# A gated recurrence beside expert layers and attention: the state's decay moved to ScalarE, and the blend scanned over three elements per batch in place of two

## The chip, the core and the metric

The kernel runs on one core of one Trainium2 chip. Its time is the device time of one execution in microseconds; of the kernel before three runs are given, and one more that was profiled. TensorE (PE; its weight loads are PEld), VectorE (DVE), ScalarE (ACT) and GpSimd (POOL) each take their instructions strictly in the order in which they are written, and wait for one another through semaphores.

## What is computed

Four layers, each added to its own input, on x of 8 batches, 256 positions, 128 features. Layers 0 and 1 are mixtures of experts (a shared part, and eight experts of which two count for each position), layer 3 is causal attention with 16 heads. Layer 2 is a recurrence over the 256 positions; its state h has 128 features for each of 8 batches:

```python
leak = 1.0 - alpha
def step(h, z_t):
    gate = jax.nn.sigmoid(h @ Wh.T + z_t @ Wz.T + b)
    h_new = jnp.tanh(h * leak + gate * z_t)
    return (h_new, h_new)
_, hs = jax.lax.scan(step, h_t, jnp.swapaxes(z, 0, 1))
```

Here z is the output of layer 1, h_t starts as the condition vector, and every h is added to x before layer 3. With sigmoid(a) = 0.5 + 0.5 tanh(a/2), gate * z is 0.5 z tanh(a/2) + 0.5 z.

## The kernel before, in words

Positions are cut into eight chunks of 32. A planner writes out, slot by slot, which unit of work each engine does; a unit is for instance one 512 wide bank of an expert's hidden layer. One step of the recurrence is woven into most slots once the first chunk has been through layers 0 and 1: after that the later chunks' expert layers run beside the steps, and the first half of attention too. What is left of attention runs behind the last step. The planner's table, the slots and the queues are the same before and after the change, but for the instructions named below.

One step t, by engine, in the order in which each writes it (line numbers of the kernel before):

- TensorE multiplies the state by Wh: the state is held as a high half hhi (16 bits, two matmuls, L987) and a rest hlo (one matmul, L990), which are added into the bank that already holds z @ Wz + b. Then it does the slot's units.
- ScalarE takes tanh of that (L734, "the gate's tanh"), into d1, does the slot's units other than the late ones, waits for the scan, and writes tanh of the scan's result twice, as hhi (L746) and as the full state hs (L747). The late units (LATE: "E", the Gelu of an expert's bank, L674; "S", an exponential of attention, L724; "K" and "Q", copies of keys and queries, L693) stand behind L747, and so ahead of the gate's tanh of the next step.
- VectorE computes hlo from hs and hhi (L1270), then the decay leak * h + 0.5 z (L1272), the first half of the slot's units, the blend as a scan (L1283), and the other half of the units. A unit that is in the middle is cut in two, half on each side of the scan.

The scan keeps a running value s and for each element sets s = d0 * s + d1. With two elements for each batch, (0, tanh) and (0.5 z, leak * h + 0.5 z), the second leaves tanh * 0.5 z + leak * h + 0.5 z, which is the argument of the new state's tanh. A copy on ScalarE for each chunk (L627, unit "Z") lays 0.5 z out in d0, which holds 128 positions at a time. GpSimd clears d0 at the start (L556).

Semaphores around a step: h_hi and h_full count L746 and L747, h_lo counts L1270, gate_pre counts L990, gate_th counts L734, decay counts L1272, blend counts L1283.

Of the kernel before, what the change touches and what calls it, by code (L numbers as in the profile page):

```python
# [19 lines left out]
F32 = mybir.dt.float32  # L20
# [3 lines left out]
ACT = mybir.ActivationFunctionType  # L24
ALU = mybir.AluOpType
AX = mybir.AxisListType

P = 128
B, T, D = 8, 256, 128
# [7 lines left out]
CHUNKS = (32,) * 8  # L37
STARTS = tuple(sum(CHUNKS[:i]) for i in range(len(CHUNKS)))
NC = len(CHUNKS)
QT = 128  # L40
# [4 lines left out]
ZR = 128  # L45
# [309 lines left out]
def chunk_of(t):  # L355
    return max(i for i in range(NC) if STARTS[i] <= t)


def build(nc, x_in, small_in, up_in, down_in, rec_in, att_in, maskr_in, out):
    parts, nth, steps, bank_of, before, hg_of, hb_of, n_slots = plan()  # L360

    with ExitStack() as ctx:
        def sb(name, shape, dt=F32):
            return ctx.enter_context(nc.sbuf_tensor(name, shape, dt))
# [7 lines left out]
        x = sb("x", [P, T * B])  # L372
# [3 lines left out]
        xsp0 = sb("xsp0", [P, 2, 2, 256], F16)  # L376
# [5 lines left out]
        sel = sb("sel", [P, E, P], F16)  # L382
# [26 lines left out]
        b2 = sb("b2", [P, 2], F16)  # L409
        leak = sb("leak", [P, 1])  # L410
        warm = sb("warm", [P, 1])
        d0 = sb("d0", [P, ZR, B, 2])
        d1 = sb("d1", [P, 2, B, 2])
        hs = sb("hs", [P, T + 1, B])
        hhi = sb("hhi", [P, 2, B], F16)
        hlo = sb("hlo", [P, 2, B], F16)
# [19 lines left out]
        wm = sb("wm", [P, B, H])  # L436
        mm = sb("mm", [P, B, H])
        mneg = sb("mneg", [P, B, H], BF16)
        eimg = sb("eimg", [P, 2, 2 * QT])

        pt = hb[:, 0:NPT, :]
        avs = hg[:, 2:4, :]
        vimgd = kq[:].rearrange("p a b n -> p (a b n)").bitcast(F32).rearrange("p (b d) -> p b d", b=B)
        on = hg[:, 0:2, :].rearrange("p a (b q) -> p (a b) q", q=QT)
        onq = sb("onq", [P, 4, P])
        rden = sb("rden", [P, 2, H])
        ob = silu[:].rearrange("p a (b q) -> p a b q", b=4)

# [3 lines left out]
        cbk = [ps("cbk0"), ps("cbk1")]  # L452
        vbk = ps("vbk")
        hid = [ps(f"hid{i}") for i in range(NHT)] + [vbk] + cbk
        vps = vbk[:, 0:2 * B]
        abk = ybk
        v_of = vx[:, 0:2 * B * H * HW].rearrange("p (t b h d) -> p t b h d", t=2, b=B, h=H)

# [56 lines left out]
        def cols(c):  # L515
            return slice(STARTS[c] * B, (STARTS[c] + CHUNKS[c]) * B)
# [28 lines left out]
        @block.gpsimd  # L545
        def _(pool):
            def split_x(c):

                n = CHUNKS[c] * B
                pool.wait_ge(in_x[c], 16)  # L550
                nc.gpsimd.tensor_copy(xsp0[:, c % 2, 0, 0:n], x[:, cols(c)]).then_inc(x_hi, 1)
                pool.wait_ge(x_hi, c + 1)
                nc.gpsimd.tensor_tensor(xsp0[:, c % 2, 1, 0:n], x[:, cols(c)], xsp0[:, c % 2, 0, 0:n],
                                        ALU.subtract).then_inc(x_split, 1)

            nc.gpsimd.memset(d0[:], 0.0).then_inc(pool_set, 1)  # L556
            nc.gpsimd.memset(gt[:], 0.0).then_inc(pool_set, 1)
            nc.gpsimd.memset(spread[:], 0.0).then_inc(pool_set, 1)
            for c in (0, 1):
                split_x(c)  # L560
            nc.gpsimd.memset(vx[:], 1.0).then_inc(pool_set, 1)
            chain = [0]

            def link(ins):

                chain[0] += 1
                ins.then_inc(pool_link, 1)
                pool.wait_ge(pool_link, chain[0])

            tts, tsc = nc.gpsimd.tensor_tensor, nc.gpsimd.tensor_scalar  # L570
            for kind, *key in parts["pool"]:
                if kind == "RG":
                    c, l = key
                    k = CHUNKS[c] * B // P
                    pool.wait_ge(dve_done, nth["dve", ("RC", c, l)])
                    if c:
                        pool.wait_ge(pe_done, nth["pe", ("GT", c - 1, l)])
                    if nth["pool", ("RG", c, l)] > 1:
                        pool.wait_ge(gates_made, nth["pool", ("RG", c, l)] - 1)
                    wide = lambda a: a.rearrange("p (k o) -> p k o", o=1).broadcast_to([P, k, E])  # L580
                    tts(pick[:, l, 0:k, :], both[:, l, 0:k, 0, :], both[:, l, 0:k, 1, :], ALU.add)
                    link(tts(gr[:, 0:k, :], sg[:, l, 0:k, :], wide(rcp2[:, l, 0:k]), ALU.mult))
                    link(tts(gr[:, 0:k, :], gr[:, 0:k, :], wide(zer2[:, l, 0:k]), ALU.add))
                    link(tts(gr[:, 0:k, :], gr[:, 0:k, :], pick[:, l, 0:k, :], ALU.mult))

                    link(nc.gpsimd.tensor_copy(g2[:, l, 0:k, 0:E], gr[:, 0:k, :]))
                    tts(g2[:, l, 0:k, E:2 * E], gr[:, 0:k, :], g2[:, l, 0:k, 0:E], ALU.subtract).then_inc(gates_made, 1)

        @block.scalar
        def _(act):  # L590
# [4 lines left out]

            act.wait_ge(in_rec, 32)
            nc.scalar.activation(warm[:, 0:1], hs[:, 0, 0:1], ACT.Gelu)

            chain = [0]

            def unit(key):
# [16 lines left out]
                elif kind == "Z":  # L618
# [5 lines left out]
                    else:  # L624
                        act.wait_ge(pool_set, 1)
                    z0 = STARTS[c] % ZR
                    nc.scalar.activation(d0[:, z0:z0 + CHUNKS[c], :, 1], x[:, cols(c)].rearrange("p (t b) -> p t b", b=B),  # L627
                                         ACT.Copy, scale=0.5).then_inc(act_done, 1)
                elif kind == "MB":

                    _, i = key
# [95 lines left out]
            for s in range(n_slots):  # L727
                t = steps.get(s)
                if t is not None:

                    act.wait_ge(gate_pre, t + 1)
                    c = chunk_of(t)
                    o = (t - STARTS[c]) * B
                    nc.scalar.activation(d1[:, t % 2, :, 0], cbk[c % 2][:, o:o + B], ACT.Tanh,  # L734
                                         scale=0.5 / RS).then_inc(gate_th, 1)

                units = parts["act"][s]
                early = [k for k in units if t is None or k[0] not in LATE]
                for key in early:
                    unit(key)  # L740
                if t is not None:

                    act.wait_ge(blend, t + 1)
                    new = vps.rearrange("p (b o) -> p b o", o=2)[:, :, 1]
                    if t + 1 < T:
                        nc.scalar.activation(hhi[:, (t + 1) % 2, :], new, ACT.Tanh).then_inc(h_hi, 1)  # L746
                    nc.scalar.activation(hs[:, t + 1, :], new, ACT.Tanh).then_inc(h_full, 1)  # L747
                for key in units:
                    if key not in early:
                        unit(key)  # L750
# [245 lines left out]
        def _(dve):  # L996
# [263 lines left out]
            for s in range(n_slots):  # L1260
# [7 lines left out]
                if t:  # L1268
                    dve.wait_ge(h_full, t)
                    tts(hlo[:, t % 2, :], hs[:, t, :], hhi[:, t % 2, :], ALU.subtract).then_inc(h_lo, 1)  # L1270
                dve.wait_ge(act_done, nth["act", ("Z", chunk_of(t))])
                stt(d1[:, t % 2, :, 1], hs[:, t, :], leak[:], d0[:, t % ZR, :, 1], ALU.mult, ALU.add).then_inc(decay, 1)  # L1272

                first = [k for i, k in enumerate(units) if i < len(units) // 2]
                rest = units[len(units) // 2:]
                cut = len(units) % 2 == 1 and rest[0][0] in HALVED
# [2 lines left out]
                if cut:  # L1279
                    unit(rest[0], 0)  # L1280
                dve.wait_ge(gate_th, t + 1)
                dve.wait_ge(decay, t + 1)
                nc.vector.tensor_tensor_scan(vps, d0[:, t % ZR].rearrange("p b o -> p (b o)"),  # L1283
                                             d1[:, t % 2].rearrange("p b o -> p (b o)"), 0.0, ALU.mult,
                                             ALU.add).then_inc(blend, 1)
                if cut:
                    unit(rest[0], 1)
# [84 lines left out]
```

## Time and profile before

| what | value |
|---|---|
| median of 3 runs | 520.59 us (519.63 to 524.53) |
| the profiled execution | 519.57 us, of which the span from the first to the last instruction is 517.8 us |
| granted TensorE clock, mean of the span | 0.968 |
| gate's tanh of the first and of the last step | 45.7 us and 373.6 us into the span |
| busy: PE, DVE, ACT, POOL | 90%, 69%, 53%, 6% |

The 256 steps take the stretch from 45.7 to 373.9 us. Ahead of it the first chunk goes through the expert layers, behind it TensorE is busy with attention (from 450 to 500 us it is busy all the time). A matmul's end is modelled, so 90% is not a full TensorE.

### The profile page before, as it was taken

Reading aid. Unit: us, or ns where it says so; the run is one execution under the profiler, and the core shown is the slowest. Engines: PE = TensorE matmul, PEld = TensorE weight load, DVE = VectorE, ACT = ScalarE, POOL = GpSimd, SP = SyncE. Lnnn points to the kernel's source line nnn. Section 1 sums busy time; section 2 is a strip of 40 time slices with the busy share of each in tenths; the row PEclk is TensorE's granted clock in tenths of the full one; section 3 lists DMA queues with packets and bytes.
Section 4 is the critical chain, followed back from the end, with each engine's and each line's share of the span. In section 5 each row is a group of like instructions: output and inputs, shape, how many; then the busy total and the mean of one; then the engine's idle time right before and its main releaser. Section 6 shows DMA issues by size and latency. Waiting matters only on the chain. (4 is left out here: it accounts for less than half of the span.)

```text
span 517.8 us, 12688 instructions
## 1 busy us (share of the span) xinstructions
PE 464.6 (90%) x4202; PEld 312.7 (60%) x4202; DVE 355.4 (69%) x1562; ACT 273.0 (53%) x1112; POOL 30.7 (6%) x108
## 2 busy tenths in 40 slices
PE   3899997888999998999998878899998799999995
PEld 2667576556676676766765335566564566766662
DVE  5766887887887888778777688877533865555501
ACT  3442644644646546455455754465668544454561
POOL 7120100000200101010000000000000000000000
PEclk9999997998999999999999978999999799999997
DMA  8400000000000000000000000000000000000000
GB/s 313 187 1 1 2 0 3 2 1 2 1 2 3 1 1 3 1 2 2 1 2 2 0 1 1 3 1 3 1 22 3 1 22 3 1 1 23 2 3 21
DMA packets 4912, 8.30 MB, mean 16 GB/s; under 512 B 496, under 2 KB 3824, under 8 KB 4720
## 3 DMA queue, kind: packets, MB, share of 16 engines
q1 hardware_dynamic: 4416, 7.23, 3.9%
q8 instruction: 35, 0.57, 0.5%
q10 hardware_dynamic: 432, 0.27, 0.2%
q14 instruction: 29, 0.24, 0.2%
HBM read 6.44 MB, written 1.05 MB: 14 GB/s over the span
## 5 line engine op out<-in xcount | busy, mean ns | idle before, releaser
L822 PE MATMUL ybk<-hg,down 128*128 128x256 f32 x352 | 97.5, 401 | 2.0 <-DVE hg L1160 1.2
L968 PE MATMUL hid<-xsp,up 128*128 128x256 f16 x672 | 94.5, 281 | 3.9 <-DVE up L1046 1.6
L734 ACT ACTIVATE d<-cbk 128x8 f32<-128x8 f32 x256 | 45.8, 179 | 96.9 <-PE cbk L990 95.7
L1283 DVE TENSOR_TENSOR_SCAN vbk<-d 128x16 f32<-128x16 f32 x256 | 51.2, 200 | 34.7 <-ACT d L734 31.4
L746 ACT ACTIVATE hhi<-vbk 128x8 f16<-128x8 f32 x255 | 44.9, 176 | 53.3 <-DVE vbk L1283 52.9
L987 PEld LDWEIGHTS cbk<-hhi,wh 128*128 128x128 f16 x512 | 38.0, 99 | 54.5 <-ACT hhi L746 45.1
L968 PEld LDWEIGHTS hid<-xsp,up 128*128 128x128 f16 x672 | 60.6, 100 | 14.2 <-ACT hb L674 2.2
L822 PEld LDWEIGHTS ybk<-hg,down 128*128 128x128 f32 x352 | 60.6, 192 | 8.9 <-DVE hg L1160 2.1
L1201 DVE TENSOR_REDUCE wm<-hid 128x2 f32<-128x256 f32 (+2 forms) x94 | 50.7, 541 | 22.0 <-PE hid L881 19.8
L987 PE MATMUL cbk<-hhi,wh 128*128 128x8 f16 x512 | 51.3, 171 | 11.1 <-ACT hhi L746 9.4
L1270 DVE TENSOR_TENSOR hlo<-hs,hhi 128x8 f16<-128x8 f32 x255 | 42.8, 168 | 24.4 <-ACT hs L747 21.2
L990 PE MATMUL cbk<-hlo,wh 128*128 128x8 f16 x256 | 45.2, 176 | 14.6 <-DVE hlo L1270 6.5
L1272 DVE SCALAR_TENSOR_TENSOR d<-hs,leak,d 128x8 f32<-128x8 f32 x256 | 56.6, 221 | 0.0
L1165 DVE TENSOR_TENSOR hg<-hb,hid 128x256 f32<-128x256 f32 (+1 forms) x110 | 50.5, 460 | 7.5 <-PE hid L808 6.7
L724 ACT ACTIVATE hb<-hid,att 128x512 f32<-128x512 f32 x60 | 40.9, 688 | 26.9 <-PE hid L932 26.3
L747 ACT ACTIVATE hs<-vbk 128x8 f32<-128x8 f32 x256 | 44.4, 173 | 0.3 <-DVE vbk L1283 0.3
L990 PEld LDWEIGHTS cbk<-hlo,wh 128*128 128x128 f16 x256 | 24.6, 96 | 30.5 <-DVE hlo L1270 23.5
L674 ACT ACTIVATE hb<-hid 128x512 f32<-128x512 f32 x64 | 38.5, 603 | 3.4 <-PE hid L968 3.2
L945 PE MATMUL ybk<-hb,vx 128*32 128x128 f32 x768 | 36.0, 282 | 1.0 <-ACT hb L724 1.0
L932 PEld LDWEIGHTS hid<-ident,mneg 128*128 128x128 bf16 x240 | 18.4, 98 | 12.2 <-issue 0.3
L808 PE MATMUL hid<-gt,sel 128*128 128x256 f16 x128 | 24.2, 274 | 0.0
L724 ACT ACTIVATE hb<-cbk,att 128x512 f32<-128x512 f32 x22 | 15.1, 687 | 16.8 <-PE cbk L932 16.8
(212 smaller groups left out, 716.1 us busy)
## 6 DMA issues: line engine op xcount, KB each, us to landing
qz<-up_in SPq DMA_DIRECT2D x3, 512.0 KB, 7.8
kp<-maskr_in SPq DMA_DIRECT2D x1, 1024.0 KB, 11.8
out_dram<-silu SPq DMA_DIRECT2D x4, 256.0 KB, 2.3
x<-x_in SPq DMA_DIRECT2D x7, 128.0 KB, 8.8
down<-down_in SPq DMA_DIRECT2D x1, 768.0 KB, 9.8
att<-att_in SPq DMA_DIRECT2D x1, 751.0 KB, 9.9
down<-down_in SPq DMA_DIRECT2D x1, 640.0 KB, 6.9
qz<-up_in SPq DMA_DIRECT2D x1, 256.0 KB, 3.8
```

What stands on the lines that cost most here:

```text
L724: nc.scalar.activation(pt[:, i % NPT, :], hid[bank_of[key]][:], ACT.Exp, bias=A("maskt", b * 2 + kb, 1), scale=SC).then_inc(act_done, 1)
L734: nc.scalar.activation(d1[:, t % 2, :, 0], cbk[c % 2][:, o:o + B], ACT.Tanh, scale=0.5 / RS).then_inc(gate_th, 1)
L746: nc.scalar.activation(hhi[:, (t + 1) % 2, :], new, ACT.Tanh).then_inc(h_hi, 1)
L747: nc.scalar.activation(hs[:, t + 1, :], new, ACT.Tanh).then_inc(h_full, 1)
L822: m = pe.matmul(ybk[l][:, 0:n], D(l, "w2" if shared else "e2", e * f + i), hg[:, hg_of[made] % NHG, i * n:i * n + n], start=first and i == ...
L968: m = pe.matmul(into, up[:, pw, a:a + P], x_part(c, l, px, slice(0, n)), start=j == 0, stop=j == 2)
L987: pe.matmul(pre, wh2[:, i, :], hhi[:, t % 2, :], start=False, stop=True, skip_group_check=True)
L990: pe.matmul(pre, wh2[:, 0, :], hlo[:, t % 2, :], start=False, stop=True, skip_group_check=True).then_inc(gate_pre, 1)
L1165: i = tts(hg[:, hg_of[key] % NHG, w], hb[:, hb_of["E", c, l, e] % NHB, w], hk[:, w], ALU.mult)
L1201: i = nc.vector.tensor_reduce(wm[:, b, a * nh + r.start:a * nh + r.stop], hk[:].rearrange("p (h k) -> p h k", h=nh)[:, r], AX.X, ALU.max)
L1272: stt(d1[:, t % 2, :, 1], hs[:, t, :], leak[:], d0[:, t % ZR, :, 1], ALU.mult, ALU.add).then_inc(decay, 1)
L1283: nc.vector.tensor_tensor_scan(vps, d0[:, t % ZR].rearrange("p b o -> p (b o)"), d1[:, t % 2].rearrange("p b o -> p (b o)"), 0.0, ALU.mult ...
```

## The change

The decay is no longer a VectorE instruction. ScalarE writes leak * h with a scaled copy, whose scale is the column leak (one number for each partition), right behind the full state's tanh, for the step that follows; since the copy reads what that tanh has just written, it waits for h_full, which the tanh itself raises. The 0.5 z that the decay added before now gets an element of its own: d0 and d1 become two planes of one ring dd, with three elements for each batch, (0, tanh), (0.5 z, 0.5 z) and (1, leak * h), and the result is the third. The copy "Z" therefore writes 0.5 z in both planes, 512 elements for each partition in place of 256. GpSimd sets the zeros and ones with two memsets of 1024 elements in place of one of 2048. At the start ScalarE makes the first decay, for which it waits until VectorE has computed leak. Two small buffers now share memory with others (eimg with xsp0, onq with sel), with no instruction added.

```diff
-        d0 = sb("d0", [P, ZR, B, 2])
-        d1 = sb("d1", [P, 2, B, 2])
+        dd = sb("dd", [P, ZR, 2, B, 3])
...
-        eimg = sb("eimg", [P, 2, 2 * QT])
+        eimg = xsp0[:].rearrange("p a r n -> p (a r n)").bitcast(F32).rearrange("p (a n) -> p a n", a=2)
...
-        onq = sb("onq", [P, 4, P])
+        onq = sel[:].rearrange("p e n -> p (e n)").bitcast(F32).rearrange("p (a d) -> p a d", d=P)
...
-        vps = vbk[:, 0:2 * B]
+        vps = vbk[:, 0:3 * B]
...
-            nc.gpsimd.memset(d0[:], 0.0).then_inc(pool_set, 1)
+            nc.gpsimd.memset(dd[:, :, 0, :, 0], 0.0)
+            nc.gpsimd.memset(dd[:, :, 0, :, 2], 1.0).then_inc(pool_set, 1)
...
+            act.wait_ge(consts, 1)
+            nc.scalar.activation(dd[:, 0, 1, :, 2], hs[:, 0, :], ACT.Copy, scale=leak[:, 0:1]).then_inc(decay, 1)
...
-                    nc.scalar.activation(d0[:, z0:z0 + CHUNKS[c], :, 1], x[:, cols(c)].rearrange("p (t b) -> p t b", b=B),
-                                         ACT.Copy, scale=0.5).then_inc(act_done, 1)
+                    z = x[:, cols(c)].rearrange("p (t o b) -> p t o b", o=1, b=B).broadcast_to([P, CHUNKS[c], 2, B])
+                    nc.scalar.activation(dd[:, z0:z0 + CHUNKS[c], :, :, 1], z, ACT.Copy, scale=0.5).then_inc(act_done, 1)
...
-                    nc.scalar.activation(d1[:, t % 2, :, 0], cbk[c % 2][:, o:o + B], ACT.Tanh,
+                    nc.scalar.activation(dd[:, t % ZR, 1, :, 0], cbk[c % 2][:, o:o + B], ACT.Tanh,
...
-                    new = vps.rearrange("p (b o) -> p b o", o=2)[:, :, 1]
+                    new = vps.rearrange("p (b o) -> p b o", o=3)[:, :, 2]
...
+                    if t + 1 < T:
+                        act.wait_ge(h_full, t + 1)
+                        nc.scalar.activation(dd[:, (t + 1) % ZR, 1, :, 2], hs[:, t + 1, :], ACT.Copy,
+                                             scale=leak[:, 0:1]).then_inc(decay, 1)
...
-                dve.wait_ge(act_done, nth["act", ("Z", chunk_of(t))])
-                stt(d1[:, t % 2, :, 1], hs[:, t, :], leak[:], d0[:, t % ZR, :, 1], ALU.mult, ALU.add).then_inc(decay, 1)
-
...
-                nc.vector.tensor_tensor_scan(vps, d0[:, t % ZR].rearrange("p b o -> p (b o)"),
-                                             d1[:, t % 2].rearrange("p b o -> p (b o)"), 0.0, ALU.mult,
+                nc.vector.tensor_tensor_scan(vps, dd[:, t % ZR, 0].rearrange("p b o -> p (b o)"),
+                                             dd[:, t % ZR, 1].rearrange("p b o -> p (b o)"), 0.0, ALU.mult,
```

How the instructions stand now on ScalarE, in two slots of the recurrence that hold a late Gelu. Before (`d` in L734's row is d1; lines of the kernel before):

```order
L747 ACTIVATE hs<-vbk 128x8
L674 ACTIVATE hb<-hid 128x512 [waits dve_done,pe_done]
L734 ACTIVATE d<-cbk 128x8 [waits gate_pre]
L746 ACTIVATE hhi<-vbk 128x8 [waits blend]
L747 ACTIVATE hs<-vbk 128x8
L674 ACTIVATE hb<-hid 128x512 [waits dve_done,pe_done]
L734 ACTIVATE d<-cbk 128x8 [waits gate_pre]
L746 ACTIVATE hhi<-vbk 128x8 [waits blend]
```

And the same place now (lines of the changed kernel; L736 is the gate's tanh, L748 and L749 write the state, L676 is the Gelu):

```order
L752 ACTIVATE dd<-hs,leak 128x8 [waits h_full]
L676 ACTIVATE hb<-hid 128x512 [waits dve_done,pe_done]
L736 ACTIVATE dd<-cbk 128x8 [waits gate_pre]
L748 ACTIVATE hhi<-vbk 128x8 [waits blend]
L749 ACTIVATE hs<-vbk 128x8
L752 ACTIVATE dd<-hs,leak 128x8 [waits h_full]
L676 ACTIVATE hb<-hid 128x512 [waits dve_done,pe_done]
L736 ACTIVATE dd<-cbk 128x8 [waits gate_pre]
L748 ACTIVATE hhi<-vbk 128x8 [waits blend]
```

One instruction is put in, L752, between the full state's tanh and the Gelu, and with it a wait that everything behind it on ScalarE shares.

VectorE in two consecutive slots and the head of a third, before (L1144 to L1149 are parts of a routing unit, L1160 is half of a shared layer's unit; the scan is printed as a SCALAR_TENSOR_TENSOR, and writes bank vbk):

```order
L1270 TENSOR_TENSOR hlo<-hs,hhi 128x8 [waits h_full]
L1272 SCALAR_TENSOR_TENSOR d<-hs,leak,d 128x8 [waits act_done]
L1144 TENSOR_SCALAR zer<-den 128x2 [waits dve_done]
L1145 TENSOR_SCALAR rcp<-den 128x2
L1146 RECIPROCAL rcp<-rcp 128x2 [waits dve_link]
L1283 SCALAR_TENSOR_TENSOR vbk<-d 128x16 [waits decay,gate_th]
L1149 SCALAR_TENSOR_TENSOR rcp<-den,rcp 128x2 [waits dve_link]
L1270 TENSOR_TENSOR hlo<-hs,hhi 128x8 [waits h_full]
L1272 SCALAR_TENSOR_TENSOR d<-hs,leak,d 128x8 [waits act_done]
L1160 SCALAR_TENSOR_TENSOR hg<-hid,silu 128x256 [waits pe_done,dve_done]
```

The same place now:

```order
L1276 TENSOR_TENSOR hlo<-hs,hhi 128x8 [waits h_full]
L1150 TENSOR_SCALAR zer<-den 128x2 [waits dve_done]
L1151 TENSOR_SCALAR rcp<-den 128x2
L1152 RECIPROCAL rcp<-rcp 128x2 [waits dve_link]
L1286 SCALAR_TENSOR_TENSOR vbk<-dd 128x24 [waits decay,gate_th]
L1155 SCALAR_TENSOR_TENSOR rcp<-den,rcp 128x2 [waits dve_link]
L1276 TENSOR_TENSOR hlo<-hs,hhi 128x8 [waits h_full]
L1166 SCALAR_TENSOR_TENSOR hg<-hid,silu 128x256 [waits pe_done,dve_done]
```

The decay is gone from between hlo and the slot's units, and the scan covers 24 elements of each partition in place of 16; nothing else has moved.

## Rows read from the trace of the kernel before

**Rows 1.** The page: busy time, share of the span and instructions of each engine.

```profile
PE 464.6 (90%) x4202; PEld 312.7 (60%) x4202; DVE 355.4 (69%) x1562; ACT 273.0 (53%) x1112; POOL 30.7 (6%) x108
```

**Rows 2.** Groups, 45.6 to 374.1 us: count | busy us, mean ns | idle before, releaser.

```profile
L1272 DVE SCALAR_TENSOR_TENSOR d<-hs,leak,d 128x8 f32<-128x8 f32 x255 | 56.4, 221 | 0.0
L1283 DVE TENSOR_TENSOR_SCAN vbk<-d 128x16 f32<-128x16 f32 x256 | 51.2, 200 | 34.7 <-ACT d L734 31.4
L734 ACT ACTIVATE d<-cbk 128x8 f32<-128x8 f32 x256 | 45.8, 179 | 96.9 <-PE cbk L990 95.7
L674 ACT ACTIVATE hb<-hid 128x512 f32<-128x512 f32 x52 | 31.5, 605 | 0.0
L724 ACT ACTIVATE hb<-hid,att 128x512 f32<-128x512 f32 x20 | 13.8, 692 | 0.0
L693 ACT ACTIVATE kp<-hid 128x512 f16<-128x512 f32 x12 | 6.9, 608 | 0.0
L693 ACT ACTIVATE fq<-hid 128x512 f16<-128x512 f32 x8 | 4.6, 608 | 0.0
```

**Rows 3.** Timeline of one step: start us, us, engine line op [idle before].

```profile
201.23 0.18 ACT L734 ACTIVATE d<-cbk 128x8 f32<-128x8 f32 x1
...
201.44 0.20 DVE L1283 TENSOR_TENSOR_SCAN vbk<-d 128x16 f32<-128x16 f32 x1 [0.40 <-ACT d L734]
...
201.67 0.18 ACT L746 ACTIVATE hhi<-vbk 128x8 f16<-128x8 f32 x1
201.74 0.17 ACT L747 ACTIVATE hs<-vbk 128x8 f32<-128x8 f32 x1
...
201.80 0.60 ACT L674 ACTIVATE hb<-hid 128x512 f32<-128x512 f32 x1
...
201.95 0.17 DVE L1270 TENSOR_TENSOR hlo<-hs,hhi 128x8 f16<-128x8 f32 x1
202.03 0.22 DVE L1272 SCALAR_TENSOR_TENSOR d<-hs,leak,d 128x8 f32<-128x8 f32 x1
...
202.17 0.16 DVE L1144 TENSOR_SCALAR zer<-den 128x2 f32<-128x2 f32 x1
202.17 0.18 PE L990 MATMUL cbk<-hlo,wh 128*128 128x8 f16 x1
...
202.39 0.18 ACT L734 ACTIVATE d<-cbk 128x8 f32<-128x8 f32 x1
```

**Rows 4.** Timeline of ScalarE at the first late exponential of the recurrence.

```profile
317.08 0.69 ACT L724 ACTIVATE hb<-hid,att 128x512 f32<-128x512 f32 x1
317.67 0.17 ACT L734 ACTIVATE d<-cbk 128x8 f32<-128x8 f32 x1
```

**Rows 5.** Groups by form, whole span: two ScalarE instructions that read SBUF, for prices.

```profile
L701 ACT ACTIVATE qz<-fq,att 128x512 f16<-128x512 f16 x16 | 10.0, 745 | 0.0
...
L645 ACT ACTIVATE sg<-th 128x16 f32<-128x16 f32 x16 | 3.5, 216 | 0.5
```

**Rows 6.** Groups by form, VectorE, 45 to 374 us: 256 and 16 elements.

```profile
L1165 DVE TENSOR_TENSOR hg<-hb,hid 128x256 f32<-128x256 f32 x92 | 38.3, 416 | 4.2 <-PE hid L808 3.5
...
L1111 DVE SCALAR_TENSOR_TENSOR sl<-th,rb 128x16 f32<-128x16 f32 x13 | 2.2, 167 | 0.0
```

**Rows 7.** Line L627 (unit Z): duration min/median/max, first and last start.

```profile
L627 ACT ACTIVATE d<-x x8: 428/431/442, 43.9 to 283.0; 128x256 f32<-128x256 f32 x8
```

**Rows 8.** Timeline of a step whose scan is late.

```profile
73.35 0.42 DVE L1165 TENSOR_TENSOR hg<-hb,hid 128x256 f32<-128x256 f32 x1 [0.16 <-PE hid L808]
73.41 0.18 ACT L734 ACTIVATE d<-cbk 128x8 f32<-128x8 f32 x1 [0.56 <-PE cbk L990]
73.69 0.19 DVE L1283 TENSOR_TENSOR_SCAN vbk<-d 128x16 f32<-128x16 f32 x1
...
73.92 0.18 ACT L746 ACTIVATE hhi<-vbk 128x8 f16<-128x8 f32 x1 [0.33 <-DVE vbk L1283]
...
74.39 0.19 PE L987 MATMUL cbk<-hhi,wh 128*128 128x8 f16 x2
```

## The prediction, made before the changed kernel had run

> **What bounds the kernel now.** I read the page first: TensorE is busy 90% of the span, VectorE 69%, ScalarE 53% [rows 1]. Shares alone would say that ScalarE has room and VectorE is worth relieving. But the steps of the recurrence wait for one another, so the next view was the groups of its stretch, 45.6 to 374.1 us [rows 2]: the gate's tanh L734 had 96.9 us of idle time before it, 95.7 of them waiting for L990. The third view was the timeline of single steps [rows 3]. What is to be seen there is a chain around four engines' ends: tanh L734 at 201.23, scan 0.21 us later, hhi 0.23 after that, hs 0.07, hlo 0.21, matmul L990 0.22, and the next tanh 0.22, at 202.39. That makes 1.16 us for a step in which nothing is late. The 255 periods between 45.7 and 373.6 us average 1.286, so the steps take 328 us, of which 296 are this bare chain and 32 are lateness of some unit. Behind the last step comes work for TensorE that waits for the last states. A microsecond that the chain gains or loses is thus one of the total.
>
> The slack matters next. The decay is not on the chain: it starts 0.08 us after hlo and the scan comes 0.57 after it [rows 3]. And in [rows 3] the Gelu L674 starts right behind hs, at 201.80, takes 0.605 and lets the next instruction start some 0.10 before its end (an exponential of 0.69 us at 317.08 lets a tanh start at 317.67 [rows 4]). ScalarE is free again at 202.30, and the chain wants it at 202.39: 0.09 us to spare.
>
> **VectorE loses the decay.** 256 instructions of 221 ns are 56.6 us less busy time (255 of them in [rows 2]); the one behind it starts 0.14 after it [rows 3], so each slot's units start 0.14 earlier. This pays only where VectorE is late for the scan or for hlo. In the timeline I count 54 scans that start over 0.22 us after their tanh, the first at 52.36 and the last at 373.87, 5.6 us late together; that, and nothing, are the bounds. [Rows 8] is the commonest kind: half a product of 0.42 us starts at 73.35, the scan comes 0.28 after its tanh, so 0.07 late, but the state's matmul L987 then starts only 0.47 after hhi, where 0.23 is usual, because TensorE is in the slot's own matmuls. The lateness of VectorE is hidden behind TensorE there. I take **-1.5 us**, nearer to nothing.
>
> **The scan gets 8 more elements.** Two ends: one pass costs (416 - 167) / (256 - 16) = 1.04 ns an element [rows 6], 8 ns for eight; a scan of 16 takes 200 ns [rows 2] where a plain instruction of 16 takes 167 [rows 6], 33 ns more, so that at most 3.1 ns an element, 25 ns for eight. I take the middle, 17 ns. It is on the chain in each step in which nothing else is late behind it; the tanh L734 was recorded as waiting for TensorE in 180 of the steps, and that many I count (their idle time is in [rows 2]). **+3.1 us** (1.5 to 4.5). The Trainium skill ("DVE: opcode table, instruction layouts, handler registers and perf-mode slots", section Datapath and trigger behaviour) says that tensor_tensor_scan runs at half throughput; by it the added element costs twice one pass, which speaks against the lower end of my range and would leave 3.1. No run here shows it yet.
>
> **ScalarE gets the decay.** Its duration: an instruction from SBUF with 16 elements takes 216 ns [rows 5], I take 0.21 for eight. Its scale is a column of numbers; the exponential, whose bias is such a column, takes 692 where the Gelu, without one, takes 605 [rows 2], so +0.085: 0.295 us, of which 0.195 hold the engine (0.10 overlap, as above). Bounds for the column's price: nothing, or what L701 shows, 745 against 608 for L693 [rows 5, 2], of which some 0.03 is its reading SBUF, so 0.11. It waits for its own engine's tanh: hs starts at 201.74, ends at 201.91, and VectorE, which waits for the same semaphore, starts at 201.95 [rows 3]. So the decay starts 0.20 after hs, and the instruction behind it 0.40 after hs, where it started 0.06 after hs: **0.34 us later**. VectorE's scan gets its decay 0.53 after hs and wants it at 0.86: not late.
>
> Where no late unit stands behind hs, the next on ScalarE is the gate's tanh, 0.65 after hs [rows 3]: the decay costs nothing, and its cover is ScalarE's idle time. That holds in 168 of 255 slots. In the other 87 I took each one's slack from the timeline (start of the tanh, less start and duration of the late unit, plus 0.10) and put down 0.34 less the slack:
> - 52 with a Gelu, the first at 52.72 and the last at 265.89 us: 35 have 0.09 to 0.10 to spare, as in [rows 3], 15 have 0.13 to 0.33, 2 have more. 10.7 us.
> - 20 with an exponential, the first in [rows 4], which has 0.00 to spare: 15 like it, 3 with 0.18 to 0.33, 2 with 0.34. 5.2 us.
> - 15 with copies of keys or queries (20 copies of 608 ns in [rows 2]): 5 with two copies, the second still running when the chain wants ScalarE, 0.34 each; 10 with one, slack 0.09 to 0.19 but for one. 3.5 us.
>
> Together **+19.5 us**. Late units are needed by TensorE no sooner than a slot later, so their own lateness adds nothing that I can price. The Trainium skill ("ScalarE: Activation LUTs", section What ACT_TABLE_LOAD costs) gives 186 ns plus 0.833 an element, 93 for a column operand and 93 of overlap: 0.286 and 0.193 for this instruction, against my 0.295 and 0.195; the sum by the page would be 0.2 us lower. Its rule for authors to use VectorE and not ScalarE for multiplications speaks against the change too.
>
> **The rest.** Copy Z with twice the elements: 431 ns now [rows 7], and 256 elements more are at most what a Gelu's 512 have over it, 0.17. Seven of eight run within the steps, between the gate's tanh and hhi, which are 0.44 apart [rows 3]; today they hold ScalarE for 0.07 + 0.33 and fit, then for 0.57: 0.13 late each, **+0.8** (0 to 1.2). The first decay, once, ahead of the first copies of weights: **+0.2**. The two memsets: GpSimd's same bytes in two instructions, an estimate of under 0.3, covered, as TensorE's first matmul on its output waits longer for VectorE: 0. Memory shared by eimg and onq: those are used in attention only, no wait added, 0.
>
> **Sum.** -1.5 + 3.1 + 19.5 + 0.8 + 0.2 = +22.1. The profiled execution took 519.57, so 541.7; it lies 1.0 under the median of the three runs, 520.59, and against that I say **542.5 us**, 4.2% slower. For this kernel 1% is about what a measurement can tell from no change.
>
> **Rivals.**
> 1. The column costs nothing, and elements little: the decay takes 0.21, the late units start 0.255 later. The same count over 87 slots gives 12.9 in place of 19.5, with 1.5 for the scan 13.9 in all: 534.5. For it: L701 differs from L693 in more than the column. Against it: 85 ns between L724 and L674. Chance 0.14.
> 2. TensorE absorbs half of the slots' loss, being 90% busy [rows 1]: 541.7 less 9.8, 532 to 533. For it: L987 late in [rows 8]. Against it: in 50 of the 72 slots with a Gelu or an exponential the slack is at most 0.10, so ScalarE is nearly the last to arrive. Chance 0.12.
> 3. Dearer: a column of 0.11 and more, decay holding 0.235: the count gives 22.8; scan 4.5, Z 1.2; total 27.2: 547. Chance 0.11.
> 4. VectorE is the bound, and not ScalarE: the whole 5.6 us of late scans comes back, and late hlo with it (54 of them, 8.0 us late together, of which 0.14 each could return: 3), while the slots' loss is not seen, because what stands behind the decay would have waited for TensorE in any case. Then 520.6 - 8.6 + 3.1 + 1.0: 516, not slower. It decides if more than 0.34 of slack lies in most of the 87 slots; the timeline shows that in 5. Chance 0.04, and 0.03 for something between it and 526.
>
> My forecast has 0.56. The range of 532 to 549 takes in rivals 1 to 3 and the bounds of the scan; some 0.16 lies outside. Chances: faster by over 1% 0.02 (a part of rival 4), within 1% 0.05, slower 0.93.
>
> **What would show it.** After: the decay with a mean near 295 ns; late units starting 0.40 after hs; the gate's tanh with idle time before it only in the 168 slots without a late unit and a few more; slots like [rows 3] 1.43 us, slots like [rows 4] some 1.5, and slots without a late unit still 1.16 to 1.18; the scan 217 ns; the last gate's tanh near 395 us, and the stretch behind it as long as before. It would be wrong if ScalarE starts the late unit without waiting for the decay's operand, or if slots without a late unit lengthen, which would put a cost on the chain that I have not counted.

## The result, and the profile after

| | before | changed |
|---|---|---|
| median, us | 522.56 (519.63 to 528.75, 4 runs) | 543.16 (542.95 to 547.08, 4 runs) |
| ratio to before, 95% interval | | 1.043 (1.034 to 1.052) |
| profiled execution, us; its span | 519.57; 517.8 | 543.06; 541.3 |
| gate's tanh, first and last, us | 45.7, 373.6 | 46.0, 396.8 |

Slower by 4.3%; 542.5 had been forecast. The ratio is that of the mean of the four changed runs, 544.1, to the mean of the others without the slow one of 528.75 us, 521.6. The page of the changed kernel, busy time and share of each engine, answers to [rows 1]:

```profile
PE 470.8 (87%) x4202; PEld 314.1 (58%) x4202; DVE 329.8 (61%) x1306; ACT 347.8 (64%) x1368; POOL 32.3 (6%) x109
```

VectorE has lost 25.6 us and ScalarE gained 74.8. TensorE does the same work in a longer span. The groups of the changed kernel in the stretch of the steps, 45.6 to 397 us, answer to [rows 2]:

```profile
L752 ACT ACTIVATE dd<-hs,leak 128x8 f32<-128x8 f32 x255 | 77.6, 304 | 8.2
L1286 DVE TENSOR_TENSOR_SCAN vbk<-dd 128x24 f32<-128x24 f32 x255 | 55.2, 216 | 76.3 <-ACT dd L736 69.0
...
L736 ACT ACTIVATE dd<-cbk 128x8 f32<-128x8 f32 x256 | 46.0, 180 | 36.4 <-PE cbk L996 20.4
...
L676 ACT ACTIVATE hb<-hid 128x512 f32<-128x512 f32 x52 | 30.0, 578 | 0.0
```

The idle time ahead of the gate's tanh has gone from 96.9 to 36.4 us, and that ahead of the scan, waiting for the tanh, has come up from 31.4 to 69.0: VectorE now waits longer for ScalarE. The same on the timeline, in a slot with a late Gelu, which answers to [rows 3]:

```profile
211.56 0.17 ACT L736 ACTIVATE dd<-cbk 128x8 f32<-128x8 f32 x1
...
211.76 0.22 DVE L1286 TENSOR_TENSOR_SCAN vbk<-dd 128x24 f32<-128x24 f32 x1 [0.62 <-ACT dd L736]
...
212.01 0.18 ACT L748 ACTIVATE hhi<-vbk 128x8 f16<-128x8 f32 x1
212.09 0.17 ACT L749 ACTIVATE hs<-vbk 128x8 f32<-128x8 f32 x1
...
212.29 0.30 ACT L752 ACTIVATE dd<-hs,leak 128x8 f32<-128x8 f32 x1
...
212.50 0.58 ACT L676 ACTIVATE hb<-hid 128x512 f32<-128x512 f32 x1
...
212.52 0.18 PE L996 MATMUL cbk<-hlo,wh 128*128 128x8 f16 x1
...
212.98 0.17 ACT L736 ACTIVATE dd<-cbk 128x8 f32<-128x8 f32 x1
```

The decay starts 0.20 us after hs and the Gelu 0.41 after hs, where it was 0.06. The Gelus themselves have become a little shorter, 578 ns in the mean where it was 605 (and the exponentials 669 for 692), which gives back some 0.03 each time. TensorE has the pre-activation ready at 212.70, but the tanh starts when the Gelu lets it, at 212.98. The step takes 1.42 us, not 1.16. With an exponential the same (compare [rows 4]), and the step takes 1.50:

```profile
353.11 0.17 ACT L736 ACTIVATE dd<-cbk 128x8 f32<-128x8 f32 x1
...
353.84 0.31 ACT L752 ACTIVATE dd<-hs,leak 128x8 f32<-128x8 f32 x1
354.04 0.67 ACT L726 ACTIVATE hb<-hid,att 128x512 f32<-128x512 f32 x1
354.61 0.17 ACT L736 ACTIVATE dd<-cbk 128x8 f32<-128x8 f32 x1
```

And copy Z, in the changed kernel's groups by form over the whole span (compare [rows 7]):

```profile
L630 ACT ACTIVATE dd<-x 128x512 f32<-128x512 f32 x8 | 7.1, 885 | 6.2 <-DVE x L1177 6.0 <-issue 0.2
```

and in one step:

```profile
79.44 0.18 ACT L736 ACTIVATE dd<-cbk 128x8 f32<-128x8 f32 x1 [0.32 <-PE cbk L996]
79.79 0.89 ACT L630 ACTIVATE dd<-x 128x512 f32<-128x512 f32 x1 [0.16 <-issue]
80.53 0.16 ACT L748 ACTIVATE hhi<-vbk 128x8 f16<-128x8 f32 x1
```

Z takes 885 ns where it took 431, and hhi starts 1.09 after the gate's tanh, not 0.44. Of the seven steps with a copy Z this one grew most, by 0.61 us, because Z starts 0.35 after the tanh; in the other six it starts 0.07 after it. In all seven it holds ScalarE for 0.73.

### The profile page after: what moved, and what is told of

Same layout as the page of the kernel before. It is cut to its first block and busy times, and to the rows that moved or that the text cites. A ratio compares the mean times of both kernels' runs of the same rounds, so it can differ in the third digit from the quotient of the medians.

```text
span 541.3 us, 12689 instructions
## 1 busy us (share of the span) xinstructions
PE 470.8 (87%) x4202; PEld 314.1 (58%) x4202; DVE 329.8 (61%) x1306; ACT 347.8 (64%) x1368; POOL 32.3 (6%) x109
## 5 line engine op out<-in xcount | busy, mean ns | idle before, releaser
L1286 DVE TENSOR_TENSOR_SCAN vbk<-dd 128x24 f32<-128x24 f32 x256 | 55.4, 216 | 76.5 <-ACT dd L736 69.3
L974 PE MATMUL hid<-xsp,up 128*128 128x256 f16 x672 | 95.6, 284 | 7.0 <-ACT hb L676 4.3
L752 ACT ACTIVATE dd<-hs,leak 128x8 f32<-128x8 f32 x255 | 77.6, 304 | 8.2
L748 ACT ACTIVATE hhi<-vbk 128x8 f16<-128x8 f32 x255 | 45.0, 177 | 53.8 <-DVE vbk L1286 53.3
L736 ACT ACTIVATE dd<-cbk 128x8 f32<-128x8 f32 x256 | 46.0, 180 | 36.4 <-PE cbk L996 20.4
L1171 DVE TENSOR_TENSOR hg<-hb,hid 128x256 f32<-128x256 f32 (+1 forms) x110 | 50.3, 458 | 10.9 <-PE hid L814 10.3
L749 ACT ACTIVATE hs<-vbk 128x8 f32<-128x8 f32 x256 | 44.2, 173 | 0.3 <-DVE vbk L1286 0.3
L676 ACT ACTIVATE hb<-hid 128x512 f32<-128x512 f32 x64 | 37.1, 581 | 3.2 <-PE hid L974 2.9
```

The costliest lines, as they stand in the source:

```text
L736: nc.scalar.activation(dd[:, t % ZR, 1, :, 0], cbk[c % 2][:, o:o + B], ACT.Tanh, scale=0.5 / RS).then_inc(gate_th, 1)
L752: nc.scalar.activation(dd[:, (t + 1) % ZR, 1, :, 2], hs[:, t + 1, :], ACT.Copy, scale=leak[:, 0:1]).then_inc(decay, 1)
L974: m = pe.matmul(into, up[:, pw, a:a + P], x_part(c, l, px, slice(0, n)), start=j == 0, stop=j == 2)
L1171: i = tts(hg[:, hg_of[key] % NHG, w], hb[:, hb_of["E", c, l, e] % NHB, w], hk[:, w], ALU.mult)
L1286: nc.vector.tensor_tensor_scan(vps, dd[:, t % ZR, 0].rearrange("p b o -> p (b o)"), dd[:, t % ZR, 1].rearrange("p b o -> p (b o)"), 0.0, A ...
```

## The experiments

Each ran beside the kernel before on the same chip; ratios are to that, with their 95% interval, and so are differences, unless another kernel is named. The kernel before took 519.42 us in median beside experiments 1 to 6, 9 and 10, and 520.33 beside 7, 8 and 11. The changed kernel itself did not run again beside them: a difference to its 543.16 us is looser than the others. Where small parts are at stake I compare the 255 periods between gate's tanhs one by one in the two timelines, by what stands behind hs.

**1. The copy alone.** Edit to the kernel before:

```diff
                     nc.scalar.activation(hs[:, t + 1, :], new, ACT.Tanh).then_inc(h_full, 1)
+                    if t + 1 < T:
+                        act.wait_ge(h_full, t + 1)
+                        nc.scalar.activation(spare[:, t % 2, :], hs[:, t + 1, :], ACT.Copy, scale=leak[:, 0:1])
```

> The kernel before, with one thing added: behind each full state's tanh ScalarE also makes the scaled copy leak * h, waiting for h_full as the changed kernel does, into a spare buffer that nobody reads. VectorE keeps its decay, the scan keeps 16 elements, unit Z its 256. Theory A (the cost is ScalarE's time ahead of the late units): 0.34 us in each of 87 slots less their slack, so 19 us over the kernel before (17 to 21), slots with a late Gelu longer by 0.25, slots without a late unit unchanged at 1.16. Theory B (the cost lies in the new layout: the longer scan, the wider copy Z and the strided ring): under 8 us over the kernel before.

Measured: 538.15, ratio 1.036 (1.034 to 1.038), 18.7 us. Period by period the steps grew by 19.1 us: 10.8 in the 52 slots with a Gelu (typically 0.24), 5.1 in the 20 with an exponential (0.33), 3.6 in the 15 with copies, and -0.4 in the 168 with nothing late. The spare copy on the timeline of this kernel:

```profile
141.95 0.17 ACT L748 ACTIVATE hs<-vbk 128x8 f32<-128x8 f32 x1
142.16 0.30 ACT L751 ACTIVATE spare<-hs,leak 128x8 f32<-128x8 f32 x1
142.36 0.58 ACT L675 ACTIVATE hb<-hid 128x512 f32<-128x512 f32 x1
142.84 0.17 ACT L735 ACTIVATE d<-cbk 128x8 f32<-128x8 f32 x1
```

Theory A holds, and theory B (under 8 us) falls: one small instruction that nobody reads costs most of what the change costs, and only where something stands behind it.

**2. The layout alone**, the decay given back to VectorE:

```diff
+                tsc(dd[:, t % ZR, 1, :, 2], hs[:, t, :], leak[:], None, ALU.mult).then_inc(decay, 1)
...
-            act.wait_ge(consts, 1)
-            nc.scalar.activation(dd[:, 0, 1, :, 2], hs[:, 0, :], ACT.Copy, scale=leak[:, 0:1]).then_inc(decay, 1)
...
-                    if t + 1 < T:
-                        act.wait_ge(h_full, t + 1)
-                        nc.scalar.activation(dd[:, (t + 1) % ZR, 1, :, 2], hs[:, t + 1, :], ACT.Copy,
-                                             scale=leak[:, 0:1]).then_inc(decay, 1)
```

> The changed kernel with the decay taken back to VectorE: dd, the scan over three elements and the wider copy Z stay, but leak * h is a VectorE multiplication at the place of the old decay, and ScalarE makes none. Theory A: only the scan (17 ns in some 180 steps, 3.1 us) and copy Z (882 ns in the changed kernel's trace where it was 431, so up to 0.45 us late in seven steps, 3 us) are left: 6 us over the kernel before (4 to 8). Theory B (the layout carries the cost): 15 us or more over the kernel before.

Measured: 524.5, ratio 1.009 (1.006 to 1.011), 5.1 us. The two halves, 18.7 and 5.1, make 23.8; the whole change is 23.5 by the spans. Within what these runs can tell they simply add. In the seven steps with a copy Z the periods grew by 2.1 us here, with no decay on ScalarE: that is the price of Z alone, but for some 0.02 of the scan in each.

**3. A constant scale**, in the changed kernel:

```diff
-                                             scale=leak[:, 0:1]).then_inc(decay, 1)
+                                             scale=0.9).then_inc(decay, 1)
```

> The changed kernel with the constant 0.9 as the scale of the decay copy in place of the column leak; what is left out is the leak of each feature. Theory A: the copy takes 0.21 us, not 0.30, the late units start 0.255 after where they did in the kernel before, not 0.34, and my count over the 87 slots falls by 6.6 us: 536 to 537. Rival (the column operand costs duration and holds nobody up, because the copy's wait for the state is what counts): no change, 543.

Measured: 536.04, ratio 1.031 (1.028 to 1.034), 7.1 us under the changed kernel; the 87 slots with a late unit are together 6.5 us shorter than there, and 6.6 had been counted. The copy takes 213 ns, not 304, and slots with a Gelu or an exponential are typically 0.09 to 0.10 shorter than in the changed kernel. The rival falls: the column of scales costs 91 ns of duration and all of it is time on the chain.

```profile
L752 ACT ACTIVATE dd<-hs x255: 212/213/215, 46.4 to 390.6; 128x8 f32<-128x8 f32 x128
```

**4. An operand that is long there**, in the changed kernel:

```diff
-                        act.wait_ge(h_full, t + 1)
-                        nc.scalar.activation(dd[:, (t + 1) % ZR, 1, :, 2], hs[:, t + 1, :], ACT.Copy,
+                        act.wait_ge(h_full, max(t, 1))
+                        nc.scalar.activation(dd[:, (t + 1) % ZR, 1, :, 2], hs[:, t, :], ACT.Copy,
```

> The changed kernel with the decay copy reading the state of one step earlier, which has long been written, so that it need not wait for the tanh in front of it; what is left out is that the decay belongs to this step's state. Theory A: the copy starts 0.06 us after hs, not 0.20, late units start 0.14 earlier, and my count over the slots falls from 19.5 to some 9: 532 to 534. Rival (ScalarE would not have started the copy sooner anyway, since the tanh in front of it holds the engine): no change, 543.

Measured: 531.1, ratio 1.023 (1.020 to 1.027), 12.1 us under the changed kernel, and a little below the 532 to 534 expected; the 87 slots are together 12.1 us shorter. On its timeline the copy starts 0.06 after hs and not 0.20:

```profile
140.80 0.17 ACT L749 ACTIVATE hs<-vbk 128x8 f32<-128x8 f32 x1
140.86 0.31 ACT L752 ACTIVATE dd<-hs,leak 128x8 f32<-128x8 f32 x1
141.05 0.60 ACT L676 ACTIVATE hb<-hid 128x512 f32<-128x512 f32 x1
```

So of the 0.35 by which a late unit was delayed, 0.15 came from the wait for ScalarE's own result, and 0.20 from the copy. Little of the 0.15 is recorded as idle time: ahead of the changed kernel's L752 that is 8.2 us for 255 copies, 0.03 each. The rest is overlap: a copy that waits cannot start while the tanh in front of it, 0.17 us long, is still running.

**5. Z on one plane**, in the changed kernel:

```diff
-            nc.gpsimd.memset(dd[:, :, 0, :, 2], 1.0).then_inc(pool_set, 1)
+            nc.gpsimd.memset(dd[:, :, 1, :, 1], 0.25)
+            nc.gpsimd.memset(dd[:, :, 0, :, 2], 1.0).then_inc(pool_set, 1)
...
-                    z = x[:, cols(c)].rearrange("p (t o b) -> p t o b", o=1, b=B).broadcast_to([P, CHUNKS[c], 2, B])
-                    nc.scalar.activation(dd[:, z0:z0 + CHUNKS[c], :, :, 1], z, ACT.Copy, scale=0.5).then_inc(act_done, 1)
+                    z = x[:, cols(c)].rearrange("p (t b) -> p t b", b=B)
+                    nc.scalar.activation(dd[:, z0:z0 + CHUNKS[c], 0, :, 1], z, ACT.Copy, scale=0.5).then_inc(act_done, 1)
```

> The changed kernel with copy Z writing one plane (256 elements), as before; what is left out is the added 0.5 z of each batch, for which a constant stands. Theory A: the 882 ns that Z takes in the changed kernel hold ScalarE between the gate's tanh and hhi, and the seven steps with one grew by 0.10 to 0.61 us, 3.2 us together; some 3 us come back, 540. Rival (those steps would be late for another unit anyway): under 1 us.

Measured: 545.93, ratio 1.049 (1.044 to 1.054): slower than the changed kernel, not faster. The total tells nothing of Z, because two other things moved. The first gate's tanh came at 48.2, not 46.0. The added memset keeps GpSimd's memsets going for longer at the start, and one VectorE instruction lasted until they had ended; TensorE's first matmul waits for what VectorE computes behind it. This kernel, and then the kernel before:

```profile
4.39 3.16 DVE L1020 CAST id<-small 128x128 f16<-128x128 f32 x1
5.59 1.81 POOL L559 MEMSET spread<- 128x2048 f16 x1
```

```profile
3.36 1.81 POOL L558 MEMSET spread<- 128x2048 f16 x1
4.06 1.26 DVE L1013 CAST id<-small 128x128 f16<-128x128 f32 x1
```

The cast ends at 7.55, the memset at 7.40; before it was 5.32 and 5.17. And TensorE's granted clock, in tenths over 40 slices of the page, here of the changed kernel and then of this one:

```profile
PEclk9999897997999999999999989899999799999997
```

```profile
PEclk9999998898999999999999867799999799999998
```

Between the 23rd and the 27th slice it was at the lower of its levels (1.2 GHz of 2.4) for 27 us here (17 of them in one stretch), for 7 there. The 32 steps that run there grew by 3.7 us. The other 223 periods are together 3.4 us shorter, but that is not the 3 us expected of Z: the seven steps with a copy Z gave back 1.9, and 0.9 came from one other step (at 131 us in the changed kernel), which there lay in a stretch at the lower clock. Not all of Z's 3 us came back, because with its 256 elements Z takes 541 ns and not the 431 of before.

**6. No decay at all**, in the kernel before:

```diff
-                stt(d1[:, t % 2, :, 1], hs[:, t, :], leak[:], d0[:, t % ZR, :, 1], ALU.mult, ALU.add).then_inc(decay, 1)
...
-                dve.wait_ge(decay, t + 1)
```

> The kernel before with the decay taken out of VectorE and done nowhere; what is left out is leak * h and 0.5 z in it (a constant stands there). The scan keeps two elements, copy Z its 256. It shows what relieving VectorE of 56.6 us is worth by itself. Theory A: 1.5 us faster than the kernel before (0.5 to 3), since TensorE covers most of VectorE's lateness. Rival (VectorE's late scans and late hlo are what the steps wait for): 5.6 to 8.6 us faster.

Measured: 525.94, ratio 1.011 (1.007 to 1.014): slower with less work, which neither theory allowed. Part of it goes with the clock: the mean granted clock of these ten runs was 0.952 to 0.972, that of the runs beside them 0.965 to 0.975; the two at 0.972 took 522.1 and 522.4 us, the kernel before at 0.972 took 519.1 to 519.9. The timelines show scans that start 0.28 us after the gate's tanh with VectorE idle, in 50 of the steps and more, where 0.21 is usual. (The 110 in the expectation of experiment 7 are too many: 107 scans are late at all, and for 58 of them VectorE stood idle.) What I had overlooked: the wait for copy Z, formerly the decay's, now stood as the first of the scan's two waits, that for the tanh as the second. Two further runs take this apart.

**7. The same with the waits in order**, the one for Z second and in eight steps only (the decay is left out as in 6; the rest of the edit to the kernel before):

```diff
                 dve.wait_ge(gate_th, t + 1)
-                dve.wait_ge(decay, t + 1)
+                if t in STARTS:
+                    dve.wait_ge(act_done, nth["act", ("Z", chunk_of(t))])
```

> As the earlier kernel without a decay on any engine, but with the scan waiting for unit Z only in the eight steps that open a chunk, and for the gate's tanh first. In the earlier kernel 110 scans came over 0.07 us late although VectorE stood idle, because there the wait on the tanh was a separate instruction of the queue in front of the scan. Theory A (that wait's form cost what the relief gave): scans start 0.21 us after the tanh again, and the time is 0 to 3 us under the kernel before, 1.5 by my prediction. Rival (a VectorE without its decay is not faster at all, or late for another reason): the same 5 us over the kernel before.

Measured: 520.16, ratio 0.999 (0.995 to 1.002). The scans are back at 0.21; the 255 periods are together 0.3 us shorter than before. By the medians VectorE's 56.6 us are worth 0.2 us. But the interval takes in my 1.5, and the runs differ in their clock: those at a mean granted clock of 0.961 and 0.962 took 520.3 to 521.2 us, the kernel before at 0.962 took 521.9 to 522.1; those at 0.973 took 516.5 to 517.1, the kernel before at 0.975 took 517.7 to 518.4. Compared so, the relief is about 1.2 us. The rival (as slow as 6) falls.

**8. Only the order of two waits**, in the kernel before:

```diff
-                dve.wait_ge(gate_th, t + 1)
                 dve.wait_ge(decay, t + 1)
+                dve.wait_ge(gate_th, t + 1)
```

> The kernel before with the scan's two waits written in the other order, the decay's first and the gate's tanh second; not an instruction more or less. Theory A (the wait written first is carried by the scan itself, the other becomes an instruction of its own in the queue, and costs 0.07 us when it is the one that ends last): scans start 0.28 us after the tanh in place of 0.21 in some 180 steps, 10 to 12 us over the kernel before. Rival (the order is indifferent): no change.

Measured: 531.19, ratio 1.024 (1.019 to 1.030), 10.9 us for two lines changing place. The scan on its timeline, against [rows 3]:

```profile
142.36 0.18 ACT L734 ACTIVATE d<-cbk 128x8 f32<-128x8 f32 x1
142.64 0.20 DVE L1283 TENSOR_TENSOR_SCAN vbk<-d 128x16 f32<-128x16 f32 x1 [0.32 <-ACT d L734]
```

0.28 after the tanh, in place of 0.21.

**9. The decay behind the late unit**, in the changed kernel (the four lines of the decay moved behind the loop over the late units):

```diff
                 for key in units:
                     if key not in early:
                         unit(key)
+                if t is not None:
+                    if t + 1 < T:
+                        act.wait_ge(h_full, t + 1)
+                        nc.scalar.activation(dd[:, (t + 1) % ZR, 1, :, 2], hs[:, t + 1, :], ACT.Copy,
+                                             scale=leak[:, 0:1]).then_inc(decay, 1)
```

> The changed kernel with the decay copy written behind the late unit and not ahead of it, everything else the same. Theory A: the late unit starts where it did in the kernel before, the copy no longer waits for the tanh, and holds ScalarE 0.20 us; the gate's tanh is late by 0.20 less the slack, 8.8 us over the 87 slots in place of 19.5: 532 to 533. Rival (the copy, ending 0.89 us after hs, now makes the scan late, which wants it at 0.86 to 0.97): no gain, or a loss of a few us.

Measured: 534.21, ratio 1.025 (1.019 to 1.030); the periods are 10.5 us shorter than the changed kernel's, those of the 87 slots 10.8, and 10.7 had been counted. The medians differ by 9.0 only: in the profiled execution the first gate's tanh came 1.2 us later, and the stretch behind the last was 1.7 us longer, with 3.4 us more of it at the lower clock. The rival falls: the copy behind the Gelu ends before the scan wants it, because the gate's tanh behind it is late as well:

```profile
144.43 0.60 ACT L676 ACTIVATE hb<-hid 128x512 f32<-128x512 f32 x1
144.91 0.31 ACT L756 ACTIVATE dd<-hs,leak 128x8 f32<-128x8 f32 x1
145.10 0.19 ACT L736 ACTIVATE dd<-cbk 128x8 f32<-128x8 f32 x1
```

**10 and 11. The decay on GpSimd**, with three elements (a multiplication) and with the old two (a multiplication and an addition). The core of the second:

```diff
+                    link(tts(half[:], hs[:, t + 1, :], leak[:].broadcast_to([P, B]), ALU.mult))
+                    tts(d1[:, (t + 1) % 2, :, 1], half[:], d0[:, (t + 1) % ZR, :, 1], ALU.add).then_inc(decay, 1)
```

> Three elements, the decay made by GpSimd (a multiplication by the column leak behind h_full), with the routing's six GpSimd instructions in two groups of three, each behind a decay. Theory A: the scan wants the decay 0.86 us after hs, GpSimd can have it there 0.5 to 0.6 after hs; the late units and VectorE are both relieved, and what is left over the kernel before is the scan and Z less what VectorE gains: +3 to +5 us, 1 to 2 under the kernel with three elements and VectorE's decay. Rival (GpSimd's decay comes after the scan wants it, or slows VectorE's instructions beside it): +8 us and more.

Measured: 523.16, ratio 1.006 (1.003 to 1.008), 1.3 us under experiment 2, where VectorE makes it; by the periods 2.3 us under it. That again is what relieving VectorE is worth, though the two ran on different chips and their intervals overlap.

> The kernel before with its two elements and copy Z, and the decay made by GpSimd in two instructions (h times leak, then 0.5 z added), the routing's GpSimd instructions in two groups of three behind it; VectorE makes none, ScalarE neither. Theory A: GpSimd starts 0.26 us after hs, takes some 0.22, 0.06 and 0.22, and the decay is there 0.84 after hs, where the scan wants it at 0.86: as the kernel before or 1 to 3 us faster (517 to 519). Rival (the decay comes late by a few hundredths in every clean step, or shares a port with VectorE): 5 to 15 us slower.

Measured: 521.15, ratio 1.003 (1.000 to 1.006). On its timeline GpSimd (the first two rows) delivers at 140.29, 0.73 after hs at 139.56, in time for a scan that comes at 0.86:

```profile
139.81 0.20 POOL L603 TENSOR_TENSOR half<-hs,leak 128x8 f32<-128x8 f32 x1 [0.68 <-ACT hs L774]
140.09 0.20 POOL L608 TENSOR_TENSOR d<-half,d 128x8 f32<-128x8 f32 x1
140.21 0.18 ACT L761 ACTIVATE d<-cbk 128x8 f32<-128x8 f32 x1
```

It takes the decay off both engines and is the best of the variants that compute everything, yet level with the kernel before. With experiment 7 this says the same twice: there is little to gain from taking the decay away from VectorE, at most one or two us.

## Why the prediction was right

Term by term; the measured parts are sums over the periods of the two timelines:

| term | forecast, us | measured, us |
|---|---|---|
| 50 of the 52 Gelu slots (no Z in the step) | 10.2 | 10.9 with the longer scan in it |
| 20 exponential slots | 5.2 | 5.5 with the longer scan in it |
| 14 of the 15 slots with key and query copies (no Z in the step) | 3.2 | 2.4 |
| the seven steps with copy Z, three of which also have a late unit | 0.8 for Z, 0.8 for the decay | 3.1 |
| 164 slots with neither: longer scan less VectorE's relief | 3.1 - 1.5, for all slots | 1.0 |
| start | 0.2 | 0.3 |
| behind the last step | 0 | 0.3 |
| sum (of parts before rounding) | 22.1 | 23.5 |

The sum is 1.4 us short of what was measured, and copy Z, 1.2 us too small, is most of that.

- **The place of the loss** was right, and is shown: experiment 1 puts it in the late slots (19.1 us of steps) and nowhere else, experiments 3, 4 and 9 take from it the column's price, the wait for its own result, and the place in the queue, each by about the amount that the count over 87 slots gave (6.6, some 10.5 and 10.7 forecast; 6.5, 12.1 and 10.8 in these slots). Rivals 2 and 4 fall with it: TensorE absorbed nearly nothing.
- **The copy's price**: 304 ns for a forecast of 295, of which 207 hold the engine for 195. That is 0.012 more for each slot than forecast, and the late units' own 0.02 to 0.03 less, which the forecast did not have, make up for it: here two small errors cancel. The column costs 91 ns by experiment 3, between my 85 and the 93 that the Trainium skill ("ScalarE: Activation LUTs", section What ACT_TABLE_LOAD costs) states. Rival 1 falls. So does rival 3: neither the copy (0.235 on the engine) nor the scan (4.5 us) was as dear as it says; only Z was dearer still.
- **The scan**: 216 ns, 16 more for eight elements, forecast 17, so 2.0 ns an element where one pass costs 1.04. That is half throughput, as the Trainium skill's page "DVE: opcode table, instruction layouts, handler registers and perf-mode slots" says in Datapath and trigger behaviour; the trace agrees. The bare step went from 1.162 to 1.183 us, 21 ns: the others are in the scan's start after the tanh, 0.214 for 0.210.
- **Mis-sized: copy Z**, 0.8 us against 2.0: the 2.1 of experiment 2 less the scan's part. The 3.1 in the table holds another 0.8, the decay's delay of a late unit in three of the seven steps, which the forecast counts among Gelus and copies. My price for 256 added elements came from instructions that write side by side (0.17 us); Z's own went up by 0.45. It was not the number of elements alone: with 256 elements on one plane of the new layout (experiment 5) Z takes 541 ns, where the old layout's 256 took 431. There the elements lie 12 bytes apart, before it was 8 (between the batches of one position). The Trainium skill ("SBUF — State Buffer", section Door 1: The DMA port swizzle (why `[64,N]` ≈ `[32,N]`)) speaks of 16-byte lines of which at least two accesses each are wanted; that fits these two numbers (at 8 bytes two elements share a line, at 12 most have one to themselves), which do not prove it.
- **VectorE's relief**, -1.5 taken between 0 and -5.6, is near the truth, and the runs do not size it closer: 0.2 us by the medians of experiment 7, 0.3 by its steps, 1.2 among runs of like clock, 1.3 to 2.3 by experiment 10 against 2. What is shown is that it is far below 5.6.
- **Copies of keys and queries**: 2.4 for 3.2. Thirteen of the fourteen slots grew as counted, by 3.15 us together. The fourteenth took 2.18 us in the kernel before, at 306.7 us, in a stretch of lower clock, and 1.43 in the changed kernel, where the clock was high. One of the 164 slots without a late unit did the reverse: 1.24 us before, 2.12 in the changed kernel, at 131.3 us and the lower clock. Without these two, -0.76 and +0.88, the rows would be 3.15 and 0.15; that their sum comes out is luck.
- **The start**: 0.3 for 0.2 is no confirmation. The term for the two memsets, put at 0 as an estimate that no run had shown, was wrong: they take from 0.73 to 3.47 us where the one took from 0.73 to 2.53, VectorE's copy into tc, held up as in experiment 5, comes at 7.95 and not 7.21, and TensorE's first matmul, which waits for it, at 8.17 and not 7.44. Of that 0.73 us only 0.3 is left at the first gate's tanh; in experiments 3, 4 and 9, which change nothing ahead of it, that tanh came at 45.6, 46.5 and 47.2, so 0.3 cannot be told from no change.

## What to carry to other kernels

An instruction's cost is its place: 0.3 us on an engine busy 53% of the time cost 18.7 us in all, because in 87 of 255 slots a long instruction stood behind it and the chain's next one behind that. Before moving work onto an engine with room, count slot by slot how much idle time lies between the end of what will be pushed back and the moment at which the chain wants the engine. And before relieving an engine, look at who is late after it when it is late: if another engine would have been late anyway, the relief is worth little (here at most one or two us for 56.6 us of work).

## What the runs showed that I had not expected

- Where an instruction has two waits, their order in the program matters. The scan starts 0.21 us after the tanh when the wait for it is written first and 0.28 when it is written second; 10.9 us over 256 steps (experiment 8). This is measured on VectorE's scan alone. In the kernel before the trace holds the second wait (for the decay, L1282) as an instruction of its own ahead of the scan, while the scan carries the first; in experiment 8 it is the wait for the tanh that stands by itself. Here the wait that ends last is better written first.
- ScalarE's wait for its own previous result delayed the copy by 0.15 us each time, seven tenths of what the copy itself held, though the profile records only 0.03 us of it as idle time (experiment 4).
- One memset more on GpSimd at the start, 1.4 us, made VectorE's copy into tc 1.7 us later (9.66 for 7.95), and the first step came 2.2 us later (experiment 5). In each of the thirteen kernels one of VectorE's first instructions, whenever it had started, ended 0.02 to 0.15 us after the last of GpSimd's first row of memsets (L558 in the kernel before); the cast of id takes 1.26 us in the kernel before, 3.16 in experiment 5, and 0.42 in the changed kernel, where the instruction behind it is the one that lasts (1.85 us for 0.35). So VectorE was held up while GpSimd set memory, by the instruction that happened to run then; no run was made to take this apart.
- TensorE's clock was granted at 1.2 GHz in stretches of 3.4 to 24 us, which did not fall alike in different kernels; the longest, 24 us in experiment 6, lies within 32 steps that grew by 2.2 us together. Differences of 1 to 3 us between such kernels are better read from the steps outside.
